# Turning 16 row tiles between adapter layers by 32x32 blocks and DRAM instead of by TensorE

## The reference

```python
# L0, for all batches
attn_out = softmax((x @ Wq) @ (x @ Wk).T / 16) @ (x @ Wv) @ Wp + bp
cms_out  = gelu(attn_out @ cW1 + cb1) @ cW2 + cb2 + one_hot(code)
modifier = gelu(concat(attn_out, cms_out) @ mW1 + mb1) @ mW2 + mb2
x = clip(x + cms_out + modifier, 0, 1)
# L1, L2, L3: adapter `role[b]` for batch b
for layer in range(3):
    h = gelu(x @ W_down[role] + b_down[role])          # 256 -> 128
    y = x + h @ W_up[role] + b_up[role]                # 128 -> 256
    x = (y - mean(y)) / sqrt(var(y) + 1e-5) * gamma[role] + beta[role]
```

## Time and profile before

| | |
|---|---|
| three executions | 358.13, 359.08, 359.75 us (median 359.08) |
| profiled execution, span from the first to the last instruction | 356.0 us |
| median less that span (start and end around it) | 3.1 us |
| TensorE busy | 343.1 us (96%), 2252 instructions |
| weight loads of TensorE | 285.6 us (80%) |
| VectorE busy | 202.6 us (57%) |
| ScalarE busy | 169.2 us (48%) |
| GpSimd busy | 59.4 us (17%) |
| DMA | 46.14 MB, 30646 packets; SP's queue 43.4% of 16 engines' span, ACT's queue 0.2% |

### The profile page before, as it was taken

The page is one execution under the profiler, slowest core; times in us unless marked ns, Lnnn a source line. Parts: engine busy times, 40 slices in busy tenths (PEclk is TensorE's granted clock), DMA queues, the critical chain, the costliest instruction groups (busy, mean ns, idle before and its releaser), DMA issues.

```text
span 356.0 us, 6665 instructions
## 1 busy us (share of the span) xinstructions
PE 343.1 (96%) x2252; PEld 285.6 (80%) x2252; DVE 202.6 (57%) x488; ACT 169.2 (48%) x338; POOL 59.4 (17%) x94
## 2 busy tenths in 40 slices
PE   7789999999999999999999989999999999999994
PEld 6577688787878888888886767877899999999962
DVE  5047366432352875466544666455489778554584
ACT  3465685453642663554336443543355554543421
POOL 2700140000040110011211111012221124100231
PEclk9999999999999999999999999999999999999999
DMA  6673799268010232310085895612766534188001
GB/s 204 197 245 125 193 117 149 20 181 176 2 57 2 61 119 60 116 34 15 17 267 147 233 263 189 207 31 74 223 148 180 155 117 116 52 276 352 19 2 45
DMA packets 30646, 46.14 MB, mean 130 GB/s; under 512 B 4779, under 2 KB 15348, under 8 KB 30612
## 3 DMA queue, kind: packets, MB, share of 16 engines
q1 hardware_dynamic: 28852, 41.72, 43.4%
q0 software_dynamic: 1392, 3.80, 3.8%
q10 hardware_dynamic: 368, 0.20, 0.2%
HBM read 43.60 MB, written 4.48 MB: 135 GB/s over the span
## 4 chain that ended last, share of the span: by engine, by line
PE 83%; SPq 5%; DMA 4%; issue 3%; ACT 2%; DVE 1%; POOL 1%; POOLq 0%; DVEq 0%
PE bank L328 12%; PE bank L330 11%; PE bank L329 11%; PE bank L1431 8%; PE bank L1436 7%; PE bank L1432 7%; PE bank L1475 4%; PE bank L1454 4%; DMA mixed_w<-packed_w 3%; PE bank L1337 2%; PE bank L1295 2%; SPq L569 2%; PE bank L1355 2%; PE bank L1506 1%; SPq L573 1%
## 5 line engine op out<-in xcount | busy, mean ns | idle before, releaser
L792 ACT ACTIVATE h_full<-bank,bias 128x512 f32<-128x512 f32 (+1 forms) x80 | 48.1, 602 | 108.7 <-PE bank L330 101.9
L1029 DVE TENSOR_TENSOR h_lo<-h_full,h_hi 128x512 fp32r<-128x512 f32 (+1 forms) x80 | 46.8, 584 | 63.6 <-ACT h_hi L796 62.3
L712 POOL TENSOR_TENSOR rstd<-moments,minus_half 128x1 f32<-128x1 f32 x39 | 21.9, 562 | 171.5 <-DVE moments L1095 171.4
L796 ACT ACTIVATE h_hi<-h_full 128x512 fp32r<-128x512 f32 (+1 forms) x80 | 43.7, 546 | 2.5
L1087 DVE TENSOR_TENSOR window_y<-bank,window_x 128x256 f32<-128x256 f32 x39 | 16.5, 423 | 38.9 <-PE bank L1454 31.6
L1431 PE MATMUL bank<-h_hi,c_hi 128*128 128x512 f32 (+1 forms) x80 | 30.4, 389 | 0.1
L1431 PE MATMUL bank<-h_hi,m_hi 128*128 128x512 f32 (+1 forms) x80 | 30.3, 387 | 0.1
L328 PE MATMUL bank<-at_hi,c_hi 128*128 128x512 f32 (+1 forms) x80 | 29.5, 368 | 0.0
L328 PE MATMUL bank<-at_hi,m_hi 128*128 128x512 f32 (+1 forms) x80 | 29.2, 365 | 0.0
L330 PE MATMUL bank<-at_lo,c_hi 128*128 128x512 f32 (+1 forms) x80 | 27.9, 348 | 0.0
L330 PE MATMUL bank<-at_lo,m_hi 128*128 128x512 f32 (+1 forms) x80 | 27.8, 348 | 0.0
(11 more groups left out here) (229 smaller groups left out, 732.9 us busy)
## 6 DMA issues: line engine op xcount, KB each, us to landing
adapter_w<-packed_w SPq DMA_DIRECT2D x48, 256.5 KB, 3.5
adapter_rows<-packed_rows SPq DMA_DIRECT2D x36, 256.0 KB, 3.7
mixed_w<-packed_w SPq DMA_DIRECT2D x12, 256.5 KB, 4.6
stage<-in_L_cond_mW SPq DMA_DIRECT2D x6, 512.0 KB, 4.8
stage<-in_L_cond_cW SPq DMA_DIRECT2D x4, 512.0 KB, 6.5
last_w<-packed_w SPq DMA_DIRECT2D x2, 769.5 KB, 6.2
up_bias<-in_L_cond_b_up SPq DMA_DIRECT2D x12, 128.0 KB, 5.3
adapter_rows<-packed_rows SPq DMA_DIRECT2D x24, 64.0 KB, 3.1
```

The source lines that it names most:

```text
L712: pool.tensor_tensor(slot.rstd[:, :], slot.moments[:, 1:2], minus_half[:, :], ALU.pow)\
L792: act.activation(h_full[:, n % 2, rows], bank[n % 2][:, rows], ACT.Gelu, bias=bias[:, b:b + 1])\
L796: act.activation(h_hi[:, n % 2, rows], h_full[:, n % 2, rows], ACT.Copy).then_inc(h_hi_ready, 1)
L1029: dve.tensor_tensor(h_lo[:, n % 2, rows], h_full[:, n % 2, rows], h_hi[:, n % 2, rows].bitcast(F32), ALU.subtract).then_inc(h_lo_ready, 1)
```

## The change

It concerns the 16 tiles of waves 1 and 2 (`SPREAD`, windows 0 to 7, layers 0 and 1; `MOVES` = 4 DRAM tiles). The tile is turned in three steps in place of L1506 and L835:

1. VectorE, in the spot of the norm, transposes `window_x` in 32x32 blocks into `block_rows` (one instruction of 128x256, two buffers). It stands behind the residual add of the other window and ahead of the low part of the hidden tile.
2. ScalarE's queue, at the half of that spot, writes the 128 KB to DRAM (`turned_blocks`).
3. ScalarE's queue, after the next hidden tile, waits until that write has landed and reads the 128 KB back so that each feature is on its partition: 128 partitions x 4 pieces of 64 numbers (256 bytes). The down product one spot later waits for it.

The down product then reads its rows with a step between pieces of 32 columns. The remaining edits join semaphores: several one-shot ones are counted on another semaphore, each wait with the matching count.

```diff
+SPREAD = WAVES[1] + WAVES[2]
+MOVES = 4
@@ build
+        turned_blocks = [nc.dram_tensor(f"turned_blocks{n}", (P, V), F32).ap() for n in range(MOVES)]
+        block_rows = sb("block_rows", [P, 2, V])
@@ schedule
         def turned(wave, spot):
-            return [(w, at // 4 + 1) for w, at in turns(wave, spot) if at % 4 == 3 and 1 <= at // 4 + 1 < LAYERS]
+            return [(w, at // 4 + 1) for w, at in turns(wave, spot)
+                    if at % 4 == 3 and 1 <= at // 4 + 1 < LAYERS and w not in SPREAD]
+        def spread(wave, spot):
+            return [(w, layer + 1) for w, layer in norms(wave, spot) if layer + 1 < LAYERS and w in SPREAD]
+        def fetched(wave, spot):
+            return spread(wave, spot - 1)
+        def blocks_of(n):
+            return window_xT[:, n % 2, :, :].rearrange("p k m -> p (k m)").rearrange("p (q k r) -> p q k r", q=Q, k=VB)
@@ scalar, after
+                for w, layer in fetched(wave, spot):
+                    n = moves[w, layer]
+                    act.wait_ge(blocks_out[n % 2], 16 * (n // 2 + 1))
+                    if n >= 2:
+                        act.wait_ge(filled[7], use["D", *moved(n - 2)] + 1)
+                    act.dma_start(blocks_of(n).rearrange("p q k r -> p q (k r)"),
+                                  turned_blocks[n % MOVES].rearrange("(q i) (f m) -> (i f) q m", q=Q, f=Q))                        .then_inc(blocks_in[n % 2], 16)
                 for w, layer in downs(wave, spot):
@@ scalar, half
+                for w, layer in spread(wave, spot):
+                    n = moves[w, layer]
+                    act.wait_ge(blocks_turned, n + 1)
+                    act.dma_start(turned_blocks[n % MOVES], block_rows[:, n % 2, :]).then_inc(blocks_out[n % 2], 16)
                 for w, layer in downs(wave, spot):
@@ vector, before
+                for w, layer in spread(wave, spot):
+                    n = moves[w, layer]
+                    dve.wait_ge(slot_of(w).x_ready, item(w, layer - 1) + 1)
+                    if n >= 2:
+                        dve.wait_ge(blocks_out[n % 2], 16 * (n // 2))
+                    dve.transpose(block_rows[:, n % 2, :].rearrange("p (f k r) -> p k f r", f=Q, k=VB),
+                                  slot_of(w).x[:, :].rearrange("p (k i f) -> p k f i", f=Q, k=VB)).then_inc(blocks_turned, 1)
@@ tensor, after
+                    elif w in SPREAD:
+                        pe.wait_ge(blocks_in[moves[w, layer] % 2], 16 * (moves[w, layer] // 2 + 1))
```

More of the change, by code:

```diff
@@ L319, in build @@
         emptied = {b: sem(f"emptied{b}") for b in (2, 3, 5, 6, 7)}
+        blocks_turned = sem("blocks_turned")
+        blocks_out = [sem(f"blocks_out{n}") for n in range(2)]
+        blocks_in = [sem(f"blocks_in{n}") for n in range(2)]
         first_w_in = sem("first_w_in")
@@ L410, in turned, with moved @@
         def turned(wave, spot):
-            return [(w, at // 4 + 1) for w, at in turns(wave, spot) if at % 4 == 3 and 1 <= at // 4 + 1 < LAYERS]
+            return [(w, at // 4 + 1) for w, at in turns(wave, spot)
[4 more added lines that the diff above has]
+            return spread(wave, spot - 1)
+        moves = {}
+        for wave in WAVES:
+            for spot in range(SPOTS):
+                for move in spread(wave, spot):
+                    moves[move] = len(moves)
+        def moved(n):
+            return next(move for move, m in moves.items() if m == n)
+        def blocks_of(n):
+            return window_xT[:, n % 2, :, :].rearrange("p k m -> p (k m)").rearrange("p (q k r) -> p q k r", q=Q, k=VB)
         def bank_of(kind, w, layer=0):
@@ L929, in _ @@
             own = own_role.to_broadcast([B, ROLES])
[L930 removed]
+            dve.tensor_tensor(own_onehot[:, :], role_id[:, :], own, ALU.is_equal).then_inc(role_row_ready, 1)
             dve.tensor_tensor(upto, role_id[:, :], own, ALU.is_le)
@@ L1466, in after @@
                     for vb in range(VB):
-                        rows = (xT[:, vb, columns(w)] if layer == 0
-                                else window_xT[:, order["T", w, layer] % 2, vb, :])
+                        rows = (xT[:, vb, columns(w)].rearrange("p (q r) -> p q r", q=Q) if layer == 0
+                                else blocks_of(moves[w, layer])[:, :, vb, :] if w in SPREAD
+                                else window_xT[:, order["T", w, layer] % 2, vb, :].rearrange("p (q r) -> p q r", q=Q))
                         down = slice(vb * KD, (vb + 1) * KD)
@@ L1471, in after @@
                             for q in range(WIN):
-                                ins = pe.matmul(bank[b][quarter(q), 0:KD], rows[:, quarter(q)], batch_w(w, layer, q)[:, down],
+                                ins = pe.matmul(bank[b][quarter(q), 0:KD], rows[:, q, :], batch_w(w, layer, q)[:, down],
                                                 start=(vb == 0), stop=(vb == VB - 1))
```

32 lines of the change are left out of this document (13 added, 19 removed).

## The result

The changed kernel took 366.71 us (median of 6 runs, 365.07 to 369.69), the kernel before 359.05 us beside it; the ratio is 1.0237, with a 95% interval of 1.0202 to 1.0271. A second set of 6 runs gave 365.46 us and 1.0233 (1.0189 to 1.0277). It is slower by 2.3%, and above the upper end of the range (363.6). Medians are of all executions, ratios are worked out from the fast ones and not from the medians, so the two can differ by some tenths of a per cent.

What follows compares the result with a forecast made beforehand. TensorE was taken as the bound, except at 205 to 214 us, where DMA engines are full. -1.3 + 2.9 - 1.32 = +0.3 us gave 359.4 us against 359.08; own range 357.8 to 361.2, 8 in 10 356.6 to 363.6.

Steps and rivals of the forecast that it cites:

- Its own sign of being wrong: Window 5's down product starting before 212.3 or after 217 us, or wave 1 losing more than 1 us.
- Wave 2 before 213 us: Windows 4 and 5's transfers meet full DMA engines: 2.9 us lost, bounds 0 and 5.4.
- The round robin: DMA engines alternate queues packet by packet: 3.8 us on top, making the read beside SP's loads 7.1 us.
- Window 5 would end last: Window 5's second-layer down product, at 212.88 us after 1.01 us idle for mixed_w, would start 2.9 us later.
- Wave 1: 105 to 180 us: eight tiles save 1.76 us, window 1's late read costs 0.5, together -1.3 us.
- h_lo's cover: VectorE's 0.5 us block transposition fits its 0.52 us idle time ahead of the hidden tile's low part: 0 cost.
- After 213 us: Rest of wave 2, TensorE full again: six tiles by 0.22 us save 1.32 us, reads cost 0.
- The joins: Joined semaphores keep each wait's releaser and stepped rows keep the column count: 0, at worst 0.2 us.
- Around the span: 3.1 us around the 356.3 us span, added to reach 359.4 us.
- The quiet transfers: Time to landing in quiet stretches: about 1.9 us for a write, 3.3 us for a read.
- The rival of reads that are slow alone: Reads of 256-byte pieces take 5.4 us even alone, down products wait: 366.5 us, chance 0.15.
- The rival of ScalarE's waits: ScalarE's wait for a write holds a hidden tile's gelu, in wave 1 too: 361.5 us, chance 0.15.

Runs made afterwards that it cites:

- whole rows: Changed kernel, its read back taking 128 rows of 1 KB instead of 512 pieces of 256 bytes, blocks not placed: 364.25 us, ratio 1.0151.
- smaller loads: Changed kernel with SP's second-layer loads of the six mixed windows cut to 64 of 513 columns: 359.82 us, ratio 1.0038.
- late reads: Kernel with 12 moves, each read and its wait for the write put at the end of ScalarE's half turn: 362.37 us, ratio 1.0118.
- writes only: Changed kernel with the 16 writes and ScalarE's waits for them but no reads; products take the blocks from block_rows: 362.88 us, ratio 1.0152.
- the joins alone: Changed kernel with no tile moved, leaving only the joined semaphores and the memory for block_rows: 359.06 us, ratio 1.0007.
- 14 moves: Changed kernel with the first tiles of windows 4 and 5 turned by TensorE, 14 tiles moved: 358.55 us, ratio 0.9997.
- first trace: First traced execution of the changed kernel, with a low clock at the start; that set's median is 366.71 us.
- second trace: Traced execution of the changed kernel run again without any edit: median 365.46 us, span 363.1 us.
- no transfers: Changed kernel with VectorE turning blocks straight into window_xT, without write, read or placing of the blocks: 357.01 us, ratio 0.9931.
- six moves: Changed kernel moving only wave 1's tiles without the first ones of windows 0 and 1: 357.87 us, ratio 1.0011.
- 12 moves: Changed kernel with the first tiles of windows 0, 1, 4 and 5 turned by TensorE, 12 tiles moved: 357.86 us, ratio 0.9980.

## Why the prediction was wrong

It forecast no change, by 3.1 us saved and 3.4 us given back. Measured were about 2 us saved and 10 given back. Its own sign of being wrong is met: window 5's down product starts at 220.60 us, behind the 217 it named.

*Wave 2 before 213 us* is the step that failed. The prediction had the place, and the term: "window 4's read goes out at about 204.2", "lands at 209.5 to 211", +2.9 us with bounds of 0 and 5.4. Measured was 10.0 us. Three parts were mis-sized or missing.
- The write of window 4. I let its read go out behind the high part as if its write had landed by then. It took 5.54 us beside the loads, where a quiet one takes 1.7 to 2.5, and the read went out at 204.84. On the clock of the kernel before, 1.1 us further on, that is 205.9, so 1.7 us late.
- The read. I priced it at 5.3 to 6.8 us by the row of 64 KB beside full engines. It took 9.6 us, and 3.9 us once an eighth of the mixed loads was left. The small pieces are some 2 us of it by one trace each; with whole rows it was still 7.6.
- The clock. 8.04 us of idle time brought TensorE to the 1.2 GHz level, and 2.0 us more went on the products behind it. No term of mine had this. Not every stall had it: behind 2.08 us idle (smaller loads) the next product ran at full speed, behind 2.59 (late reads) and 3.30 (writes only) it didn't.

*The round robin.* The rule of the Trainium skill ("DMA: Bandwidth & Descriptors", Queues, rings and completion order) that I weighed and left out of the sum, each DMA engine going round its queues packet by packet, made 7.1 us by my estimate. The four traces have 6.5 to 9.6 us on either side of it. That the packets of both queues are mixed agrees with it. Its estimate has no place for the 2 us and more without a packet, and the counts are no steady one to one: 224 against 107 in 210 to 211 us, 38 against 160 in 207 to 208. Of the other rule of the Trainium skill ("DMA: Bandwidth & Descriptors", Specifications), pieces below 512 B miss line rate, nothing shows in quiet stretches: 2.6 us is the median with 256 B and with 1 KB.

*Window 5 would end last* (212.88 plus 2.9). It was window 4. Window 5's product starts 6.1 us behind it without a wait, and that wait of 1.01 us for `mixed_w` was no fixed feature to build on: with the joins alone the product starts 4.34 us behind window 4's without any, with 14 moves it waits for 0.62.

*Wave 1*: forecast -1.3 us, measured -0.65 against the joins. I had 0.5 us of lateness, at window 1. It came at window 0, and smaller: write issued 126.08, read 130.15, product 133.69 in the first trace, 0.25 us late, and 0.13 in the second, behind writes of 4.0 us; nothing shows for window 1. VectorE was priced at 0 and wasn't: 0.63 us per tile, just over my bound of 0.6, and 0.50 us of TensorE's waiting for a `window_x` queued behind it. I named h_lo's cover and not this second instruction behind the transposition.

The other part is in the premise: TensorE busy in 74.94 of 75 us, so the time is a sum of its instructions. At two tiles it isn't. The weight load ahead of a product on `h_hi`, with the joins alone and in the second trace, and the one ahead of the product on `pd` in the second trace:

```profile
145.20 0.19 PEld L1469 LDWEIGHTS bank<-h_hi,m_hi 128*128 128x128 f32 x1
144.90 0.19 PEld L1469 LDWEIGHTS bank<-h_hi,m_hi 128*128 128x128 f32 x1 [0.49 <-ACT h_hi L816]
161.30 1.86 PEld L1375 LDWEIGHTS bank<-pd,xr 128*128 128x128 f32 x16 [0.31 <-DVE pd L1046]
```

The transposition filled the time in which TensorE would have waited for ScalarE's high part. Without it TensorE waits: the step from the product before is 0.46 us and not 0.23, and from one down product to the next it takes 8.13 us (141.47 to 149.60) where it took 8.14 with the joins (141.76 to 149.90). The wait for VectorE's `pd` takes as much again. Both rows are in the kernels with no transfers and with six moves too. The sum of the second trace now closes: -1.76 + 2 x 0.22 + 0.49 + 0.13 = -0.70, against -0.65.

*After 213 us*: forecast -1.32, measured -1.2. *The joins*: 0, as forecast. *Around the span*: 1.8 us (357.26 with a span of 355.4) and not 3.1, which had set a short traced execution against a median; it is in both kernels alike.

*The quiet transfers*: 2.4 or 2.5 and 2.6 us against my 1.9 and 3.3. The rival of reads that are slow alone gave 366.5 us, next to the result, and is refuted: a right number by a wrong mechanism. The rival of ScalarE's waits (361.5 us) is a real mechanism, shown by the kernel with writes only at 362.88 us and covered by the read's wait in the changed kernel. I had taken the rivals as alternatives; here they lie on each other at one place.

What would have led there: the view that gave had 64 KB at 5.6 us beside full engines. Write and read are in a row, so the way is twice such a transfer, 11.2 us, where 7.0 us lie between the write's issue (199.28) and the due time of the product (207.38 in the kernel with the joins, less 1.1). That makes the product 4.2 us late, half of what it was before the low clock. I took the quiet price for the first half.

No version that computes the whole beat the kernel before by more than the measurement tells; the best is that with 12 moves, 0.9980 (0.9938 to 1.0022). The kernel with no transfers, which leaves the placing out, has its interval below 1 (0.9907 to 0.9955).

## What to carry to other kernels

A trip through DRAM is two transfers in a row and each is priced by the traffic of its own moment, so look for the one tile whose trip meets the full queue: two tiles of 16 made all of the loss. Taking 0.22 us from the bound engine pays only if neither a wait nor a longer order on a neighbour comes back in its place; even free transfers returned 2.0 of 3.5 us. TensorE was busy in 99.9% of wave 1's stretch, and still at two places of eight it waited for a neighbour as soon as 0.22 us was taken from it. A stall of TensorE like the one of 8 us here is to be priced with the slow products behind it, and a wait that a longer wait covers is still there when the longer one is taken away.

## What the runs showed of the hardware

- A 128 KB write to DRAM on ACT's queue took 1.7 to 2.5 us in quiet stretches and 5.5 to 9.7 us beside full DMA engines (share about 1, 250 to 355 GB/s). A read of 128 KB in 512 pieces of 256 bytes took 2.1 to 2.6 us quiet, about as long as one of 128 rows of 1 KB (medians of 2.6 us), and 6.5 to 9.6 us beside the loads.
- Beside SP's loads ACT's queue had no packet for over 2 us behind the issue of the read (205 to 207 us), then 625 in 5 us with SP's going on.
- A block transposition of 128x256 on VectorE took 618 to 682 ns; that of 32x128 took 303.
- TensorE stood still from 206.47 us; the granted clock of 207 to 209 us is 0.91 on average and 0.50 from 209 us on, and, TensorE at work again since 214.51 us, it is 0.53 in 217 to 219 us and 1.00 behind that.
- Some executions have a stretch of low clock in 14 to 26 us, 3 of 17 traced, and one of them lost 4.5 us by it; 9 of 17 have one in 58 to 70 us.
